# Loads of the attention output sweep double-buffered, one weight split hoisted, a third of the weight quantization moved into the gate/up sweep

## The reference

```
xn = layernorm(x)
# branch 1
q, k, v = xn @ Wq.T, xn @ Wk.T, xn @ Wv.T
kvt  = cumsum(k * v, axis=tokens) * sqrt(D) / seq
att  = (q * kvt) @ Wo.T
# branch 2, weights rounded to {-1, 0, 1} * mean|w|, activations to 8-bit steps
gate = sigmoid(bitlinear(xn, w_gate)); up = bitlinear(xn, w_up)
ffn  = bitlinear(gate * up, w_down)
out  = x + att + ffn
```

## Time and profile before

| | us |
|---|---|
| median of 2 runs | 11056.22 |
| lowest and highest | 10805.73 and 11306.7 |
| the profiled execution | 10805.73 |
| its span on the slowest core (core 4) | 10803.9 |
| spans of the other cores | 10750.0 to 10794.8 |
| TensorE, matmuls busy | 7280.3 |
| DVE busy | 3984.8 |
| ACT busy | 685.4 |

### The profile page before, as it was taken

The page is one execution under the profiler, slowest core; times in us unless marked ns, Lnnn a source line. Parts: engine busy times, 40 slices in busy tenths (PEclk is TensorE's granted clock), DMA queues, the critical chain, the costliest instruction groups (busy, mean ns, idle before and its releaser), DMA issues.

```text
span 10803.9 us, 91885 instructions; the slowest of 8 cores (10750.0 to 10803.9 us)
## 1 busy us (share of the span) xinstructions
PE 7280.3 (67%) x32530; PEld 3349.1 (31%) x32530; DVE 3984.8 (37%) x4921; ACT 685.4 (6%) x1193; POOL 16.3 (0%) x20
## 2 busy tenths in 40 slices
PE   2999995466665665765366468999999444445555
PEld 1444442232232332322133233444444222222222
DVE  4355554334334344234322222222222444443333
ACT  3000001100000000000000000000010000000000
POOL 0000000000000000000000000000000000000000
PEclk9999997688887887887688788999999666677777
DMA  1455553124334334334322222121221444444544
GB/s 67 129 170 170 165 162 110 47 95 140 108 102 137 105 110 136 97 105 133 113 63 63 78 63 87 70 85 70 83 71 54 145 140 144 141 163 152 164 163 160
DMA packets 521848, 1230.85 MB, mean 114 GB/s; under 512 B 44082, under 2 KB 240818, under 8 KB 498866
## 3 DMA queue, kind: packets, MB, share of 16 engines
q1 hardware_dynamic: 376242, 1006.81, 29.5%
q10 hardware_dynamic: 142848, 201.39, 5.1%
q0 software_dynamic: 2304, 16.78, 0.8%
HBM read 1006.70 MB, written 218.10 MB: 113 GB/s over the span
## 4 chain that ended last, share of the span: by engine, by line
PE 57%; DMA 19%; DVE 16%; issue 3%; ACT 2%; ACTq 1%; DVEq 1%; SPq 0%; POOL 0%; POOLq 0%
PE pb L419 9%; PE pb L422 9%; PE pb L426 8%; PE pb L839 8%; PE pb L834 8%; PE pb L1009 5%; DMA S<-wd_s 4%; DMA wd_s<-A 4%; DMA A<-vhat_s 3%; DMA wg_s<-A 3%; DMA wu_s<-A 3%; DVE A L291 3%; PE pb L977 2%; PE pb L751 2%; PE pb L754 2%
## 5 line engine op out<-in xcount | busy, mean ns | idle before, releaser
L419 PE MATMUL pb<-S,A 128*128 128x512 bf16 x5120 | 1982.9, 387 | 1221.5 <-DVE A L403 779.4
L422 PE MATMUL pb<-S,A 128*128 128x512 bf16 x5120 | 1981.8, 387 | 0.0
L426 PE MATMUL pb<-S,A 128*128 128x512 bf16 x5120 | 1977.8, 386 | 0.0
L834 PE MATMUL pb<-S 128*128 128x512 bf16 x4096 | 1555.6, 380 | 20.7 <-DMA S<-wu_s 20.7
L839 PE MATMUL pb<-S 128*128 128x512 bf16 x4096 | 1555.3, 380 | 0.0
L419 PEld LDWEIGHTS pb<-S,A 128*128 128x128 bf16 x5120 | 508.1, 99 | 1866.8 <-issue 1286.3
L1009 PE MATMUL pb<-S 128*128 128x512 bf16 x4096 | 941.3, 391 | 141.9 <-DMA S<-wd_s 127.6
L977 PE MATMUL pb<-id32s,A 128*128 128x128 f32 x1024 | 248.2, 422 | 1072.4 <-DVE A L966 1072.4
L426 PEld LDWEIGHTS pb<-S,A 128*128 128x128 bf16 x5120 | 508.4, 99 | 631.6 <-issue 47.0
L422 PEld LDWEIGHTS pb<-S,A 128*128 128x128 bf16 x5120 | 507.2, 99 | 621.5 <-issue 39.1
L860 DVE SCALAR_TENSOR_TENSOR A<-pb,tSCU,A 128x512 f32<-128x512 f32 x256 | 192.2, 751 | 1334.1 <-ACT A L853 1334.1
(11 more groups left out here) (102 smaller groups left out, 4397.1 us busy)
## 6 DMA issues: line engine op xcount, KB each, us to landing
S<-wd_s SPq DMA_DIRECT2D x128, 2048.0 KB, 8.9
A<-wg SPq DMA_DIRECT2D x256, 512.0 KB, 4.8
A<-wu SPq DMA_DIRECT2D x256, 512.0 KB, 4.8
A<-wd SPq DMA_DIRECT2D x256, 512.0 KB, 5.3
h_s<-A ACTq DMA_DIRECT2D x256, 256.0 KB, 2.0
A<-h_s SPq DMA_DIRECT2D x128, 512.0 KB, 3.6
A<-xm SPq DMA_DIRECT2D x48, 1024.0 KB, 5.2
A<-wk SPq DMA_DIRECT2D x32, 1024.0 KB, 7.8
```

What stands on the lines that cost most here:

```text
L419: e.matmul(pb[c][:, :], whi[p][:, dt * 128:(dt + 1) * 128], S1[:, mv:mv + 512], start=s, stop=False))
L422: e.matmul(pb[c][:, :], whi[p][:, dt * 128:(dt + 1) * 128], S2[:, mv:mv + 512], start=False, stop=False))
L426: e.matmul(pb[c][:, :], wlo[p][:, dt * 128:(dt + 1) * 128], S1[:, mv:mv + 512], start=False, stop=s))
L834: e.matmul(pb[pr * 2][:, :], S1[:, stat:stat + 128], wg_sl[sl][:, dt * 512:(dt + 1) * 512], start=s, stop=p))
```

## The change

It has three parts.

- In stage 3 the k split of the next iteration is called together with its q split, ahead of `quant_step`, in place of after the q sweep.
- `quant_step` does 16 units per iteration in stage 3 (all of gate and up). The 128 units of down move to stage 5: 8 units at the end of each block `fc`, behind `load_gu(fc + 2)`.
- In stage 4 vs_hi and vs_lo get a second buffer, and the 32 loads of iteration `gi + 1` are issued at the start of iteration `gi`, on across the change of column pair. The second buffer lies in A16 where qb_buf and the compare results are, which are not in use in stage 4 any more.

```diff
             if e + 1 < NE:
                 next_split = stream_weight_split(wq_d, e + 1, 0)
-            quant_step((len(q_units) + NE - 1) // NE)
+                next_ksplit = stream_weight_split(wk_d, e + 1, 1)
+            quant_step((2 * len(q_units) // 3 + NE - 1) // NE)
...
-            st_k = stream_weight_split(wk_d, e, 1)
+            st_k = next_ksplit if next_ksplit is not None else \
+                stream_weight_split(wk_d, e, 1)
...
             for ttg in range(NTTG):
-                wait("sync", smm, pstate.get("vs_free", 0))
-                for et in range(NE):
-                    stVR.dma(vs_hi[...], vhat_d[0, et, :, ttg * 256:...])
-                    stVR.dma(vs_lo[...], vhat_d[1, et, :, ttg * 256:...])
-                wait_all("tensor", stVR)
+                gi = pi * NTTG + ttg
+                par2 = gi % 2
+                if gi == 0:
+                    ...
+                ngi = gi + 1
+                if ngi < len(fc_pairs) * NTTG:
+                    npar = ngi % 2
+                    nttg = ngi % NTTG
+                    wait("sync", smm, pstate.get("vs_free_%d" % npar, 0))
+                    for et in range(NE):
+                        stVR.dma(vs_hi_sl[npar][...], vhat_d[0, et, :, nttg * 256:...])
+                        stVR.dma(vs_lo_sl[npar][...], vhat_d[1, et, :, nttg * 256:...])
+                    pstate["vs_toks_%d" % npar] = stVR.all_toks()
+                for tok_ in pstate["vs_toks_%d" % par2]:
+                    wait_t("tensor", tok_)
...
-                pstate["vs_free"] = smm.c
+                pstate["vs_free_%d" % par2] = smm.c
                 prep_step(n_prep_per_iter)
...
             wgu_free[sl] = smm.c
             load_gu(fc + 2)
+            quant_step(max(1, (len(q_units) // 3 + NFC - 1) // NFC))
+        quant_step(len(q_units))
```

More of the change, by code:

```diff
@@ L563, in build_program @@
         next_split = None
+        next_ksplit = None
         for e in range(NE):
@@ L616, in build_program @@
                 next_split = stream_weight_split(wq_d, e + 1, 0)
-            quant_step((len(q_units) + NE - 1) // NE)
+                next_ksplit = stream_weight_split(wk_d, e + 1, 1)
+            quant_step((2 * len(q_units) // 3 + NE - 1) // NE)
         ph3_mm = smm.c
         phase_barrier()
-        quant_step(len(q_units))
         wo_in = A32[:, 0:2048]
@@ L630, in build_program @@
         NSL = D // QW
-        vs_hi = A16[:, 0:NE * 256]
-        vs_lo = A16[:, NE * 256:2 * NE * 256]
+        vs_hi_sl = [A16[:, 0:NE * 256], A16[:, 2 * NE * 256:3 * NE * 256]]
+        vs_lo_sl = [A16[:, NE * 256:2 * NE * 256],
+                    A16[:, 3 * NE * 256:4 * NE * 256]]
         NTTG = NT // 2
@@ L728, in build_program @@
             for ttg in range(NTTG):
-                wait("sync", smm, pstate.get("vs_free", 0))
-                for et in range(NE):
[L731 to L734, removed]
-                wait_all("tensor", stVR)
+                gi = pi * NTTG + ttg
+                par2 = gi % 2
+                vs_hi = vs_hi_sl[par2]
+                vs_lo = vs_lo_sl[par2]
+                if gi == 0:
+                    wait("sync", smm, pstate.get("vs_free_%d" % par2, 0))
+                    for et in range(NE):
+                        stVR.dma(vs_hi[:, et * 256:(et + 1) * 256],
+                                 vhat_d[0, et, :, ttg * 256:(ttg + 1) * 256])
+                        vs_tok = stVR.dma(
+                            vs_lo[:, et * 256:(et + 1) * 256],
+                            vhat_d[1, et, :, ttg * 256:(ttg + 1) * 256])
+                    pstate["vs_toks_%d" % par2] = stVR.all_toks()
+                ngi = gi + 1
[3 more added lines that the diff above has]
+                    wait("sync", smm, pstate.get("vs_free_%d" % npar, 0))
+                    for et in range(NE):
+                        stVR.dma(vs_hi_sl[npar][:, et * 256:(et + 1) * 256],
+                                 vhat_d[0, et, :, nttg * 256:(nttg + 1) * 256])
+                        stVR.dma(vs_lo_sl[npar][:, et * 256:(et + 1) * 256],
+                                 vhat_d[1, et, :, nttg * 256:(nttg + 1) * 256])
+                    pstate["vs_toks_%d" % npar] = stVR.all_toks()
+                for tok_ in pstate["vs_toks_%d" % par2]:
+                    wait_t("tensor", tok_)
                 wait("tensor", svv, pair_split_done)
@@ L749, in build_program @@
                             op("tensor", lambda e, sb_h=sb_h, bkk=bkk, wb=whi_b,
-                               s=(et == 0):
-                               e.matmul(pb[bkk][:, :], vs_hi[:, sb_h:sb_h + 128],
+                               vh=vs_hi, s=(et == 0):
+                               e.matmul(pb[bkk][:, :], vh[:, sb_h:sb_h + 128],
                                         S2[:, wb:wb + 512], start=s, stop=False))
-                            op("tensor", lambda e, sb_h=sb_h, bkk=bkk, wb=wlo_b:
-                               e.matmul(pb[bkk][:, :], vs_hi[:, sb_h:sb_h + 128],
+                            op("tensor", lambda e, sb_h=sb_h, bkk=bkk, wb=wlo_b,
+                               vh=vs_hi:
+                               e.matmul(pb[bkk][:, :], vh[:, sb_h:sb_h + 128],
                                         S2[:, wb:wb + 512], start=False,
@@ L757, in build_program @@
                             lam = (lambda e, sb_h=sb_h, bkk=bkk, wb=whi_b,
-                                   s=(et == NE - 1):
+                                   vl=vs_lo, s=(et == NE - 1):
                                    e.matmul(pb[bkk][:, :],
-                                            vs_lo[:, sb_h:sb_h + 128],
+                                            vl[:, sb_h:sb_h + 128],
                                             S2[:, wb:wb + 512], start=False,
```

## The result

| | before | changed |
|---|---|---|
| median of all runs, us | 10821.9 (12 runs) | 11275.32 (14 runs) |
| lowest and highest, us | 10781.03 and 11370.15 | 10851.73 and 11447.16 |
| ratio of whole times | | 1.0067 (95% interval 1.0043 to 1.009) |

The changed kernel is slower by 0.7%: no difference by the 2% that the prediction took as the limit of what can be told, and a small loss by the ratio's own interval.

A forecast was written before the change was run, and what follows sets the result against it. Limits differ by stage: TensorE is busy 2009 of 3208 us in stage 3, 1770 of 1772 in stage 5. Terms -387 - 122 + 600 = +91 us on 10805.7 give about 10895 us, range 10700 to 11090.

The forecast's parts named there:

- Stage 3: Eight fewer units and the earlier k split save 387 us (bounds 320 to 440); ACT's q copy stays late behind stores.
- -10.1 + 2.2: Stage 3, per iteration: k load and split ahead of the units cost 10.1 us; an earlier k sweep gains 2.2.
- Stage 4: Loads issued an iteration ahead remove the vhat_s wait, saving 122 us (bounds 60 to 155); the second unit's wait stays.
- Stage 5: Units at block ends cost 600 us (bounds 390 to 824), 39 us in each of blocks 0 to 13.
- the 7.6 us per iteration: Stage 4: the vhat_s wait removed in each of 14 iterations, 106 us in all.
- The sum: Whole kernel: -387 - 122 + 600 = +91 us, 0.8% more, forecast as no measurable difference; chance 0.62.
- I sum against the lower, which is the one whose stages I can see: Whole time: the sum was added to the profiled execution's 10805.7 us, not the median of 11056 or the other run's 11306.7.
- Only the k split held the k sweep: Stage 3 rival: hoisting the split frees the sweep wholly, 10410 us, -3.7%; chance 0.06 shared with the gaps rival and top-of-bounds gains.
- Hidden in DVE's gaps: Stage 5 rival: units fit DVE's 5.10 us gaps at cost near 0, about 10300 us, -4.7%; within the shared 0.06.
- Slower by over 2%: Stage 5 rival: each unit's store wait is 3.41 us, stage 5 costs 824, kernel 11120 us, +2.9%; chance 0.17.
- The unit loads are not held: Stage 5 rival: unit loads do not wait for the weight loads, cost 390 us, kernel 10687 us, -1.1%; chance 0.15.
- each block would be like block 14: Stage 5 lower bound: without waiting for the 4.2 MB, 15 blocks cost 24 us each plus 30, 390 us.

The follow-up runs named there:

- The move alone: Kernel before with only the 128 down units moved to stage 5's block ends; stage 3 period 167.4 to 169.1 us, execution 10897.24 us.
- the hoist alone: Kernel before with only the k split called ahead of the units, 24 units staying in stage 3; period 206.1 to 208.2 us against 200.5 to 202.5.
- the spread units: Changed kernel with stage 5's units one per second tile and stage 3's 16 as 8 and 8 between sweeps; median 9709.13 us, ratio 0.8983.
- the units first: Changed kernel with the 8 units called ahead of load_gu at a block's end; stage 5 at 2256 to 2272 us, 115 less than the changed kernel.

## Why the prediction was right or wrong

**The mechanisms.** All three were as the prediction put them. Stage 3: ACT's q copy behind the stores is late next. The move alone, the hoist alone and the spread units show it from three sides (168, 207 and 142.5 us). The hoist is a loss, by about the 8 us per iteration that the prediction's terms make of it (-10.1 + 2.2): 7 to 8 us beside 16 units, 5.7 beside 24. Stage 4: the vhat_s wait goes, the wait for the second unit stays. Stage 5: DVE first waits for a load behind 4 MB, then for stores, TensorE from two tiles on.

**The terms.** Stage 3 was given 387 us and gave 412 (375 + 37). The move alone takes 33 us off a period (201.3 to 168.4 on the mean of the cores) where the prediction's terms give 29.8 + 1.8, and behind the last scan 37 went in place of 32; the hoist is as sized.

Stage 4 was given 122 and gave 148 on core 4: 133 in the 14 periods and 13 at the change of pair, where 106 and 15.6 had been given. The step that was mis-sized is the 7.6 us per iteration; 9.5 were measured. It counted the wait alone and put the quicker restart into the bounds, though it was in the row (the ninth matmul at 0.64), and that is worth 1.4 us each time; another 0.4 is a shorter wait for the second unit (211.5 us in place of 217.3 over 16).

Stage 5 was given 600 and took 614: units from E + 16.7 and not 18.3, an end at E + 47.5 and not 48.3, fourteen holes of 37.6 on the mean where 36.8 had been given, and one of 23.3 where the 24 us of its block leave 22. Two small sums of this term do not come out of their parts: 0.45 + 15.6 is E + 16.05 and not 16.2, and from the last subtraction's end 0.5 + 0.7 + 0.75 leads to E + 50.25 and not 50.6. The trace has 2.35 us for this last piece (6199.62 to 6201.97), which is what the 50.6 stands for.

The sum was 91 us, the two spans differ by 48, and the ratio makes it 0.67% of 10806, 72 us. That the net came this close is luck in part: three terms of 412, 148 and 614 us were off by 25, 26 and 14 us, the first two in favour of the change and the third against it.

**What was wrong.** The predicted time and its range, 10895 and 10700 to 11090, do not hold the median of all runs, 11275. The step that failed is the one after the sum: "I sum against the lower, which is the one whose stages I can see". The two runs shown lay 500 us apart, and the prediction named that and then built the range from the bounds of its terms alone, with nothing for which of the two a median would fall to. The runs showed that it can be the upper: nine of the 14 executions took 11030.89 us or more, and the median fell among them, 380 us above the predicted time; the other five took 10851.73 to 10916.94, on both sides of it. The profile could not tell how many would fall where, but two runs so far apart were a reason to widen the range.

**The rivals.** "Only the k split held the k sweep": refuted by the hoist alone (+5.7 us in place of -56). "Hidden in DVE's gaps": not for units in a row, and true to 2.6 us as soon as they stand between tiles, so the prediction's reason against it was right. "Slower by over 2%", with a store wait of 3.41 us in every cycle: the mean is 1.5 us (172.9 / 112). "The unit loads are not held": they are held by their own queue. Its price of 390 us, though, was wrong as well: where the loads did not wait, with the units first, stage 5 still cost 2264 - 1764 = 500 (mean of cores 0 to 3), because "each block would be like block 14" left out that the 4 MB then run beside the stores.

**What stays open.** Cores 0 and 1 of the kernel before pass stage 4 in 1216 us and the others in 1242 to 1264, so the gain of stage 4 differs from core to core between about 100 and 150 us. The difference lies in the periods (65 us on core 0, 68 on core 4), and both waits are shorter there: vhat_s 5.8 to 6.5 us in the four rows of core 0 that show it against 6.9 to 8.5 on core 4, the second unit 13.0 on the mean against 13.6. With the move alone it is cores 2 to 5 that take 1212 to 1218 us. Why the loads of some cores land earlier is not shown. Whether the down units had to leave stage 3 at all was not tried either: all 24 spread between the sweeps of stage 3 may cost as little as the 16. That the changed kernel without its hoist would be the faster by 110 us is worked out from the move alone; it was not run.

## What to carry to other kernels

On an engine that works its list in order, the cost of side work is where it stands and not how much it is: eight units in a row between two tiles cost some 39 us, the same eight one by one between the tiles next to nothing (2.6 us in the whole stage). Before an instruction is hoisted or moved, look at every queue on which the thing it waits for is issued, stores on ACT among them, and ask which of two things that end together is left. And a move from a stage where TensorE waits to a stage where it does not is a gain only if the moved work falls into gaps that its own engines have there.

## What the runs showed of the hardware that I had not expected

- A 512 KB load issued on GpSimd's queue 5 us behind 4 MB on SP's landed in 7.4 us, ahead of the second 2 MB, which then took 19.0 us in place of 14.8; issued on SP's own queue it took 14.6 us and landed behind them.
- The order of loads costs in both directions: with the 4 MB out of the way of the loads, a store's longest wait rose from 3.7 to 6.6 us.
- The price of a restart scatters: behind holes of 36 to 40 us in stage 5 of the changed kernel 1 to 14 matmuls came 0.43 us apart before the spacing fell to 0.22. In stage 4 it was 7 to 14 where the wait for vhat_s stood between the transposes and the matmuls, and 1 to 9 where the matmuls followed the transposes at once.
